# Graph network kernel: in the second network's pass the edge's part is put into the ring first, the gather adds the node's row to it, and ScalarE rectifies from the ring

## The chip, the core and the metric

The kernel runs on one core of one Trainium2 chip. The metric is the device time of one execution in microseconds (us). A core has five engines that matter here: TensorE (PE, with its weight loads as PEld), VectorE (DVE), ScalarE (ACT), GpSimd (POOL), and SyncE (SP), which here only issues DMAs. Sixteen DMA engines move the data.

## What is computed

Four graph networks run one after the other over 3125 nodes (128 features) and 50000 edges, sorted by destination. The change concerns the second one alone:

```
combined = jnp.concatenate([x[row], ef], axis=1)
msg = jax.nn.relu(combined @ Wn1 + bn1) @ Wn2 + bn2
out = jax.ops.segment_sum(msg, col, num_segments=x.shape[0])
return out + x
```

The product with `Wn1` is split in two. The node's half, `x @ Wn1[0:128] + bn1`, is a table in DRAM with a row for each node (`table`). The edge's half, `ef @ Wn1[128:]`, was computed during earlier passes and lies in DRAM by edge (`edge_part`). So each edge's message is relu(table[src] + edge_part), summed by destination; `Wn2` is applied to the sums afterwards.

## The kernel before

Edges are taken in tiles of 128, which makes 391 tiles, and four tiles make a quad (98 tile quads). A destination block is 128 nodes, and an edge tile that touches two blocks is used in two steps, so there are 416 steps in 104 step quads. All loops are unrolled, and the order is written out by hand for each engine; engines meet through semaphores (`arrived`, `mixed`, `evac`, `quad_done`, `onehot_ready`, `ring_in`, `gathered`).

The ring is a part of SBUF with 60 places, one for each tile, and every place has two halves of 128 floats. In the pass of the second network the engines do this:

- POOL (`gathers`, L479) issues one indirect DMA for each tile: it fetches 128 rows of `table`, 512 bytes each, into the first half of the tile's place. After every fourth tile it may hand over quads (`hand_over`, L470 to L475): it waits until the four gathers of a quad have landed, waits for the quad's edge load as well (`joins`, L1188), and increments `arrived`. With `rest=4` it mostly hands over the quad before the one that it has just issued; after every fourth quad, 16 tiles, it hands over the one just issued too, and stands until that has landed.
- SP (L1200) loads four tiles of `edge_part` at a time, 256 KB, into the second halves. Load k waits until quad k-8 is handed over and the place is free.
- DVE makes the one-hot matrices of a quad's destinations (L455, one instruction of 128x512) and, two quads behind that, adds the two halves of a place into `hidden` (`add`, L1209 to L1218: four instructions at L1216). Its increment of `mixed` also frees the places in the ring, for POOL (`freed`, L1185) and for SP.
- ACT rectifies a quad from `hidden` into `relu_h` in one instruction of 128x512 (L1232) and increments `evac`.
- PE adds a quad's one-hots to the degree counts (L510), one quad ahead, and multiplies relu_h with the one-hots into the block sums in PSUM (L1254).

Of the kernel before, what the change touches and what calls it, by code (L numbers as in the profile page):

```python
# [96 lines left out]
def build(nc, A, out):  # L97
    ctx = ExitStack()
    with ctx:
# [365 lines left out]

        def gathers(pool, tab, width, freed, joins=None, rest=4):

            handed = [0]

            def hand_over(k):  # L470

                pool.wait_ge(gathered[k % U].sem, gathered[k % U].at(64 * (k // U) + 16 * min(4, EDGE_TILES - 4 * k)))
                if joins is not None:
                    joins(pool, k)
                pool.sem_inc(arrived.sem, 1)  # L475
            for t in range(EDGE_TILES):
                if t % 4 == 0 and t >= RING:
                    freed(pool, (t - RING + 3 + NB - 1) // 4)
                pool.indirect_dma_start(ring[:, ds(t % RING * 2 * H, width)], None, tab,  # L479
                                        bass.IndirectOffsetOnAxis(ap=idx_s[:, t:t + 1], axis=0)).then_inc(gathered[t // 4 % U].sem, 16)  # L480
                if t % 4 == 3:
                    done = t // 4 + 1
                    for k in range(handed[0], done if done % rest == 0 else done - 1):
                        hand_over(k)
                        handed[0] = k + 1
            for k in range(handed[0], TILE_QUADS):
                hand_over(k)
# [12 lines left out]
        def step_need(eng, n):  # L500

            return eng.value_load(need_i[0:1, ds(n, 1)], min_val=1, max_val=TILE_QUADS)
# [675 lines left out]
        if STAGE >= 2:  # L1178
# [3 lines left out]
            with nc.Block() as block:  # L1182
                @block.gpsimd
                def _(pool):
                    def freed(pool, n):  # L1185
                        pool.wait_ge(mixed.sem, mixed.at(n + 1))

                    def joins(pool, k):  # L1188
                        pool.wait_ge(ring_in[k % HALF].sem, ring_in[k % HALF].at(16 * (k // HALF + 1)))
                    gathers(pool, table, H, freed, joins, rest=4)  # L1190

                @block.sync
                def _(sp):
                    pairs = ring.rearrange("p (r c) -> p r c", c=2 * H)
                    for k in range(TILE_QUADS):
                        if 4 * k >= RING:
                            sp.wait_ge(mixed.sem, mixed.at((4 * k - RING + 3 + NB - 1) // 4 + 1))
                        if k >= HALF:
                            sp.wait_ge(arrived.sem, arrived.at(k - HALF + 1))
                        sp.dma_start(pairs[:, 4 * k % RING:4 * k % RING + 4, H:2 * H],  # L1200
                                     edge_part[4 * k:4 * k + 4, :, :].rearrange("t e f -> e t f")).then_inc(ring_in[k % HALF].sem, 16)

                @block.vector
                def _(dve):
                    def join(i, q, first):
                        if not (first and q < 2):
                            add(i * QUADS + q - 2, (q - 2) % QUADS, not (first and q < 4))

                    def add(n, q, reused):  # L1209
                        r = 4 * (q % 2)  # L1210
                        slot_regs, slots, partners = step_slots(dve, n * 4, 4, behind=(0, H))
                        dve.wait_ge(arrived.sem, step_need(dve, n) + arrived.base)
                        if reused:
                            dve.wait_ge(evac.sem, evac.at(n - 1))
                        for c in range(4):
                            sum_ = dve.tensor_tensor(hidden[:, r + c, :], arena[:, ds(slots[c], H)], arena[:, ds(partners[c], H)], ALU.add)  # L1216
                        release(dve, slot_regs)
                        sum_.then_inc(mixed.sem, 1)  # L1218
                    onehots(dve, None, join, home=deep)
                    for q in range(2, QUADS):  # L1220
                        add(ALL_QUADS - QUADS + q, q, True)

                @block.scalar
                def _(act):
                    def body(i, first):
                        for q in range(QUADS):
                            n = i * QUADS + q
                            r = 4 * (q % 2)
                            act.wait_ge(mixed.sem, mixed.at(n + 1))
                            if n >= RELUS:  # L1230
                                act.wait_ge(quad_done.sem, quad_done.at(n - RELUS + 1))
                            act.activation(relu_h[:, 4 * (n % RELUS):4 * (n % RELUS) + 4, :], hidden[:, r:r + 4, :], ACT.Relu).then_inc(evac.sem, 1)  # L1232
                    trips(act, body)
                    take_totals(act)

                @block.tensor
# [23 lines left out]
                    add_totals(pe)  # L1260
            gather_pass_over()
            totals_over()
            mixed.base += ALL_QUADS
            evac.base += ALL_QUADS
            for k in range(TILE_QUADS):
                ring_in[k % HALF].base += 16
# [1128 lines left out]
```

## Time and profile before

| | us |
|---|---|
| three runs | 6473.24, 6457.61, 6471.04 (median 6471.04) |
| the profiled execution | 6410.16, its span 6408.1 |
| PE busy in the span | 3293.9 (51%) |
| POOL busy | 3221.9 (50%) |
| DVE busy | 2162.9 (34%) |
| ACT busy | 1006.4 (16%) |
| the pass of the second network, first gather to last | 2000.03 to 2566.8 of the span |

The profiled execution is one of several, and here it lies 61 us below the median of the timed ones. The shares are means over passes with different limits. An engine at half of the span can still be the one that sets the pace of a stretch, since register, semaphore and DMA-issuing instructions of the queues are not counted as busy, and the small gap between two instructions isn't either.

### The profile page before, as it was taken

To read this page: it belongs to the slowest core of one execution; us is meant where nothing else is said; L and a number is where in the kernel's file an instruction comes from. 1 tells how busy PE (TensorE), PEld (TensorE's weight loads), DVE (VectorE), ACT (ScalarE), POOL (GpSimd) and SP (SyncE) were. 2 spreads that over 40 slices of the span, in tenths; PEclk is the share of its full clock that TensorE was granted. 3 is DMA by queue.
4 is the path that set the end of the run, shared out by engine and by line. 5 is a ranking of instruction groups with operands and counts; after the bars stand their busy time and mean duration, and the time that the engine had idled before them with its cause. 6 is when DMAs were issued, how large, how long until landed. Compare 5 with 4: busy or idle time off the path is not lost. (4 is left out here: it accounts for less than half of the span.)

```text
span 6408.1 us, 51881 instructions
## 1 busy us (share of the span) xinstructions
PE 3293.9 (51%) x13857; PEld 2295.6 (36%) x13857; DVE 2162.9 (34%) x5075; ACT 1006.4 (16%) x2209; POOL 3221.9 (50%) x3406
## 2 busy tenths in 40 slices
PE   5554677767774555643463344643324356333263
PEld 3333455545552333332343232233324322333153
DVE  3222322232224222411121114533338544333485
ACT  0000322232222111200010002400004324000063
POOL 4665466546663666366646663046650320566403
PEclk7676777677776777755565556755557677555586
DMA  2111334333432332211131116976653579766453
GB/s 61 46 47 40 88 98 101 98 82 99 101 99 79 91 90 82 107 46 47 46 131 47 46 46 251 427 239 185 182 149 111 149 287 427 204 187 184 118 148 95
DMA packets 630965, 826.34 MB, mean 129 GB/s; under 512 B 93075, under 2 KB 510341, under 8 KB 618133
## 3 DMA queue, kind: packets, MB, share of 16 engines
q1 hardware_dynamic: 480117, 492.37, 22.9%
q0 software_dynamic: 120608, 276.12, 16.2%
q10 hardware_dynamic: 29952, 54.54, 2.9%
q8 instruction: 116, 1.90, 0.1%
q14 instruction: 172, 1.41, 0.1%
HBM read 470.63 MB, written 352.04 MB: 128 GB/s over the span
## 5 line engine op out<-in xcount | busy, mean ns | idle before, releaser
L479 POOL DMA_INDIRECT arena<-table,idx_s x3128 | 3001.8, 960 | 2353.5 <-issue 1095.5
L751 PE MATMUL ps<-arena,work 128*128 x4160 | 985.9, 378 | 1050.0 <-issue 934.9
L751 PEld LDWEIGHTS ps<-arena,work 128*128 128x128 f32 x4160 | 824.8, 274 | 1317.4 <-issue 1170.3
L1965 PE MATMUL ps<-arena,work 128*128 x1664 | 412.7, 426 | 693.7 <-issue 488.2
L1965 PEld LDWEIGHTS ps<-arena,work 128*128 128x128 f32 x1664 | 359.1, 317 | 748.6 <-issue 530.1
L459 DVE TENSOR_SCALAR work<-iota_row,dl_s,w_s 128x128 f32<-128x128 f32 x1248 | 350.4, 358 | 454.6 <-issue 349.4
L455 DVE TENSOR_TENSOR work<-ps,dl_s 128x512 f32<-128x512 f32 x208 | 143.8, 692 | 926.5 <-issue 617.0
L1934 DVE TENSOR_TENSOR arena<-arena,ps 128x128 f32<-128x128 f32 x832 | 182.7, 281 | 741.9 <-issue 500.0
L929 DVE SCALAR_TENSOR_TENSOR arena<-ps,vecs,arena 128x256 f32<-128x256 f32 x208 | 100.6, 484 | 893.9 <-issue 435.9
L1832 PE MATMUL ps<-arena,work 32*128 32x512 f32 x1600 | 299.1, 876 | 97.5 <-DVE work L1859 44.2
L510 PE MATMUL ps<-work,picks 128*104 128x512 f32 x416 | 313.4, 842 | 46.2 <-issue 42.8
L1863 DVE COPY arena<-ps 128x1024 f32<-128x1024 f32 x200 | 238.6, 1221 | 271.0 <-DMA table<-arena 164.8
L1254 PE MATMUL ps<-work,arena 128*128 128x128 f32 x832 | 173.5, 373 | 248.6 <-ACT arena L1232 153.7
L1654 POOL DMA_INDIRECT sorted_x<-work,pos_i x50 | 48.6, 973 | 479.8 <-DVE work L1747 465.2
L1254 PEld LDWEIGHTS ps<-work,arena 128*128 128x128 f32 x832 | 148.4, 267 | 382.4 <-ACT arena L1232 231.5
L863 PE MATMUL ps<-arena 128*128 128x128 f32 x832 | 212.3, 400 | 83.9 <-DVE arena L929 41.7
L1850 ACT ACTIVATE arena<-ps 128x1024 f32<-128x1024 f32 x200 | 198.1, 1022 | 309.7 <-DMA table<-arena 187.0
L1216 DVE TENSOR_TENSOR arena<-arena 128x128 f32 x416 | 94.7, 288 | 414.3 <-issue 245.1
L2145 PE MATMUL ps<-arena,onehot 128*128 128x128 f32 x1664 | 209.4, 280 | 21.7 <-DVE arena L2125 17.0
L863 PEld LDWEIGHTS ps<-arena 128*128 128x128 f32 x832 | 164.8, 278 | 123.0 <-DVE arena L929 64.2
L857 PE MATMUL ps<-arena 128*128 128x256 f32 x416 | 193.3, 560 | 28.9 <-ACT arena L897 25.0
L2145 PEld LDWEIGHTS ps<-arena,onehot 128*128 128x128 f32 x1664 | 194.7, 191 | 36.2 <-issue 30.7
(331 smaller groups left out, 3539.5 us busy)
## 6 DMA issues: line engine op xcount, KB each, us to landing
table<-arena SPq DMA_DIRECT2D x96, 2048.0 KB
onehot<-col_rows ACTq DMA_DIRECT2D x208, 256.0 KB
values<-arena SPq DMA_DIRECT2D x832, 64.0 KB
arena<-values SPq DMA_DIRECT2D x208, 256.0 KB
arena<-table,idx_s POOLq DMA_INDIRECT x3128
arena<-edge_times SPq DMA_DIRECT2D x208, 128.0 KB
edge_part<-arena SPq DMA_DIRECT2D x208, 128.0 KB
table<-arena SPq DMA_DIRECT2D x50, 512.0 KB
```

Source lines behind the costliest of these rows:

```text
L459: is_dst = dve.tensor_scalar(home[:, at + c, :], iota, dl_s[:, ds(j + c, 1)], weight[:, ds(j + c, 1)], ALU.is_equal, ALU.mult)
L479: pool.indirect_dma_start(ring[:, ds(t % RING * 2 * H, width)], None, tab, bass.IndirectOffsetOnAxis(ap=idx_s[:, t:t + 1], axis=0)).then_i ...
L510: mm = pe.matmul(quad_sums, picks[:, ALL_QUADS - n:2 * ALL_QUADS - n], deep[:, 4 * (n % DEEP):4 * (n % DEEP) + 4, :].rearrange("p c e -> p ...
L751: mm = pe.matmul(accf[:, ds(b, P)], o, arena[:, ds(slot, H)], start=False, stop=False, skip_group_check=True)
L857: pe.matmul(self.half_b, self.We2, self.hid[:, r, :], start=True, stop=True, skip_group_check=True).then_inc(turned.sem, 1)
L863: mm = pe.matmul(self.half_a[:, c * P:(c + 1) * P], self.ef[:, r, c * P:(c + 1) * P], self.Wn1b, start=True, stop=True, skip_group_check=True)
L1254: mm = pe.matmul(accf[:, ds(b, P)], relu_h[:, (i * U + u) % (4 * RELUS), :], o, start=False, stop=False, skip_group_check=True)
L1832: mm = pe.matmul(ps[:, 4 * kv + g, :], (value_ring if kv else key_ring)[rows, b % 2, :], (pair_v if kv else pair_k)[rows, half * 16:(half ...
L1850: act.activation(rows32[:, m % 3, :, kv * H:kv * H + 64].rearrange("p t (g c) -> p g t c", g=2), ps[:, 4 * kv:4 * kv + 2, :].rearrange("p ...
L1863: dve.tensor_copy(rows32[:, m % 3, :, kv * H + 64:(kv + 1) * H].rearrange("p t (g c) -> p g t c", g=2), ps[:, 4 * kv + 2:4 * kv + 4, :].re ...
L1965: mm = pe.matmul(ps[:, n % 8, c * P:(c + 1) * P], across_ring[:, n % DEEP, c * P:(c + 1) * P], Qn_flat[:, ds(b, P)], start=True, stop=True)
L2145: mm = pe.matmul(accf[:, ds(b, P)], o, msgs[:, 4 * q + c, :], start=False, stop=False, skip_group_check=True)
```

## The change

The halves change their order of arrival. SP now loads the edge's part into the first half of a place. POOL waits for that load before the first gather of the quad, and each gather is an indirect DMA that adds the table's row to what lies there (`compute_op: ALU.add`). Its hand-over waits for the gathers alone. DVE's adds, `hidden` and the signal `mixed` are gone from this pass; after each quad's one-hots DVE calls `release_steps`, which waits for the tile quad that a step quad needs and increments `step_ready`. ACT loads the four slot addresses of a quad into registers and rectifies straight from the ring, in four instructions of 128x128 in place of one of 128x512. `evac` now frees the places.

```diff
         def gathers(pool, tab, width, freed, joins=None, rest=4):
+            adds = {} if joins is None else {"compute_op": ALU.add}
...
                 pool.wait_ge(gathered[k % U].sem, gathered[k % U].at(64 * (k // U) + 16 * min(4, EDGE_TILES - 4 * k)))
-                if joins is not None:
-                    joins(pool, k)
                 pool.sem_inc(arrived.sem, 1)
             for t in range(EDGE_TILES):
                 if t % 4 == 0 and t >= RING:
                     freed(pool, (t - RING + 3 + NB - 1) // 4)
+                if t % 4 == 0 and joins is not None:
+                    joins(pool, t // 4)
                 pool.indirect_dma_start(ring[:, ds(t % RING * 2 * H, width)], None, tab,
-                                        bass.IndirectOffsetOnAxis(ap=idx_s[:, t:t + 1], axis=0)).then_inc(gathered[t // 4 % U].sem, 16)
+                                        bass.IndirectOffsetOnAxis(ap=idx_s[:, t:t + 1], axis=0), **adds).then_inc(gathered[t // 4 % U].sem, 16)
...
                     def freed(pool, n):
-                        pool.wait_ge(mixed.sem, mixed.at(n + 1))
+                        pool.wait_ge(evac.sem, evac.at(n + 1))
...
-                            sp.wait_ge(mixed.sem, mixed.at((4 * k - RING + 3 + NB - 1) // 4 + 1))
+                            sp.wait_ge(evac.sem, evac.at((4 * k - RING + 3 + NB - 1) // 4 + 1))
                         if k >= HALF:
                             sp.wait_ge(arrived.sem, arrived.at(k - HALF + 1))
-                        sp.dma_start(pairs[:, 4 * k % RING:4 * k % RING + 4, H:2 * H],
+                        sp.dma_start(pairs[:, 4 * k % RING:4 * k % RING + 4, 0:H],
...
-                    onehots(dve, None, join, home=deep)
-                    for q in range(2, QUADS):
-                        add(ALL_QUADS - QUADS + q, q, True)
+                    def then(i, q, first):
+                        release_steps(dve, i * QUADS + q)
+                    onehots(dve, None, then, home=deep)
...
-                            act.activation(relu_h[:, 4 * (n % RELUS):4 * (n % RELUS) + 4, :], hidden[:, r:r + 4, :], ACT.Relu).then_inc(evac.sem, 1)
+                    for n in range(ALL_QUADS):
+                        slot_regs, slots = step_slots(act, n * 4, 4)
+                        act.wait_ge(step_ready.sem, step_ready.at(n + 1))
+                        if n >= RELUS:
+                            act.wait_ge(quad_done.sem, quad_done.at(n - RELUS + 1))
+                        for c in range(4):
+                            rectified = act.activation(relu_h[:, (4 * n + c) % (4 * RELUS), :], arena[:, ds(slots[c], H)], ACT.Relu)
+                        rectified.then_inc(evac.sem, 1)
+                        release(act, slot_regs)
```

On POOL, at the start of the pass, the queue before has eight gathers without a wait, and the waits for gathers and for edge loads stand together:

```order
L479 DMA arena<-table,idx_s 128x128 x8
L479 DMA arena<-table,idx_s 128x128 [waits gathered0,ring_in0]
L479 DMA arena<-table,idx_s 128x128 x3
L479 DMA arena<-table,idx_s 128x128 [waits gathered1,ring_in1]
L479 DMA arena<-table,idx_s 128x128 x3
L479 DMA arena<-table,idx_s 128x128 [waits gathered2,ring_in2,gathered3,ring_in3]
L479 DMA arena<-table,idx_s 128x128 x7
```

The same place of the changed kernel, where L481 is the gather:

```order
L481 DMA arena<-table,idx_s 128x128 [waits ring_in0]
L481 DMA arena<-table,idx_s 128x128 x3
L481 DMA arena<-table,idx_s 128x128 [waits ring_in1]
L481 DMA arena<-table,idx_s 128x128 x3
L481 DMA arena<-table,idx_s 128x128 [waits gathered0,ring_in2]
L481 DMA arena<-table,idx_s 128x128 x3
L481 DMA arena<-table,idx_s 128x128 [waits gathered1,ring_in3]
L481 DMA arena<-table,idx_s 128x128 x3
L481 DMA arena<-table,idx_s 128x128 [waits gathered2,gathered3,ring_in4]
```

Each quad's first gather now waits for its own quad's edge load; the waits for landed gathers stand where they stood, and their number is the same.

On DVE in the middle of the pass, one turn of the loop before (L256 and L502 load the slot addresses and the need into registers):

```order
L256 TENSOR_LOAD slot_i
L502 TENSOR_LOAD need_i
L502 ISA x2
L1212 REGISTER_ALU
L1216 REGISTER_ALU [waits evac,arrived]
L1216 TENSOR_TENSOR arena<-arena 128x128
L1216 REGISTER_ALU
...
L1216 TENSOR_TENSOR arena<-arena 128x128
L455 TENSOR_TENSOR work<-iota_row,dl_s 128x512
```

and one turn in the changed kernel:

```order
L455 TENSOR_TENSOR work<-iota_row,dl_s 128x512 [waits arrived,quad_done]
L504 TENSOR_LOAD need_i
L504 ISA x2
L548 REGISTER_ALU [waits onehot_ready]
```

The one-hots (L455) now come right behind the wait for `arrived`, where the four adds stood; before, they came behind the adds.

On ACT, before and in the changed kernel, two quads:

```order
L1232 ACTIVATE arena<-arena 128x512 [waits quad_done,mixed] x94
```

```order
L256 TENSOR_LOAD slot_i
L1219 ACTIVATE arena<-arena 128x128 [waits quad_done,step_ready]
L1219 ACTIVATE arena<-arena 128x128 x3
L256 TENSOR_LOAD slot_i
L1219 ACTIVATE arena<-arena 128x128 [waits quad_done,step_ready]
```

One instruction a quad has become one load of addresses and four instructions.

## Rows read from the trace of the kernel before

**Rows 1.** The page: span, engines' busy us, DMA share by queue, all gathers.

```profile
span 6408.1 us, 51881 instructions
...
PE 3293.9 (51%) x13857; PEld 2295.6 (36%) x13857; DVE 2162.9 (34%) x5075; ACT 1006.4 (16%) x2209; POOL 3221.9 (50%) x3406
...
q0 software_dynamic: 120608, 276.12, 16.2%
...
L479 POOL DMA_INDIRECT arena<-table,idx_s x3128 | 3001.8, 960 | 2353.5 <-issue 1095.5 <-POOLq L1784 477.2 <-DMA arena<-table,idx_s 305.7
```

**Rows 2.** Stretches of this pass: busy us of each engine, PE clock, DMA share.

```profile
2050.00:2150.00 100.00, 57.68 (x182) 32.54 (x180) 27.20 (x90) 11.34 (x18) 70.42 (x70) 0.71 0.32 91
...
2250.00:2350.00 100.00, 54.96 (x180) 32.17 (x180) 28.68 (x95) 11.82 (x19) 68.42 (x68) 0.73 0.31 90
```

**Rows 3.** Groups on POOL, DVE, ACT in this pass: busy, mean ns | idle before.

```profile
L479 POOL DMA_INDIRECT arena<-table,idx_s x391 | 394.2, 1008 | 245.9 <-issue 153.7 <-POOLq L1082 73.3 <-DMA arena<-table,idx_s 18.9
...
L1216 DVE TENSOR_TENSOR arena<-arena 128x128 f32 x416 | 94.7, 288 | 414.3 <-issue 245.1 <-POOLq L475 167.5 <-ACT arena L1232 1.2
L455 DVE TENSOR_TENSOR work<-iota_row,dl_s 128x512 f32<-128x512 f32 x104 | 70.8, 683 | 2.6 <-PEq L1082 2.6
L1232 ACT ACTIVATE arena<-arena 128x512 f32<-128x512 f32 x104 | 65.5, 630 | 511.1 <-issue 335.3 <-DVE arena L1216 175.8
...
L987 ACT ACTIVATE work<-ps 128x128 f32<-128x128 f32 x1 | 0.3, 278 | 0.4 <-PE ps L965 0.4
```

**Rows 4.** Timeline of POOL: start us, us, idle before in brackets.

```profile
2251.09 0.95 POOL L479 DMA_INDIRECT arena<-table,idx_s  x1 [0.30 <-issue]
2252.35 1.31 POOL L479 DMA_INDIRECT arena<-table,idx_s  x1 [0.31 <-issue]
2256.04 1.09 POOL L479 DMA_INDIRECT arena<-table,idx_s  x1 [2.39 <-issue]
```

**Rows 5.** Timeline of POOL and DVE together, eight us further on.

```profile
2262.44 0.94 POOL L479 DMA_INDIRECT arena<-table,idx_s  x1 [0.30 <-issue]
...
2262.64 0.90 DVE L1216 TENSOR_TENSOR arena<-arena 128x128 f32 x4 [5.72 <-POOLq L475]
2263.45 0.68 DVE L455 TENSOR_TENSOR work<-iota_row,dl_s 128x512 f32<-128x512 f32 x1
...
2263.69 1.27 POOL L479 DMA_INDIRECT arena<-table,idx_s  x1 [0.30 <-issue]
```

**Rows 6.** POOL groups of two later passes: rows of 512 B, rows of 1 KB.

```profile
L479 POOL DMA_INDIRECT arena<-table,idx_s x391 | 370.5, 948 | 182.1 <-issue 143.0 <-DMA arena<-table,idx_s 23.8 <-remote 10.6
...
L479 POOL DMA_INDIRECT arena<-table,idx_s x391 | 372.9, 954 | 437.6 <-POOLq L1784 238.3 <-issue 127.6 <-DMA arena<-table,idx_s 50.4
```

**Rows 7.** One-hots (L455) of the later pass with 512 B rows.

```profile
L455 DVE TENSOR_TENSOR work<-ps,dl_s 128x512 f32<-128x512 f32 x103 | 71.2, 691 | 464.0 <-issue 322.6 <-POOLq L475 74.1 <-remote 59.2
```

**Rows 8.** Start of the pass: POOL, SP, then DMA share of two stretches.

```profile
2000.03 0.95 POOL L479 DMA_INDIRECT arena<-table,idx_s  x1 [73.29 <-POOLq L1082]
...
1999.39 12.81 SPq L1200 DMA_DIRECT2D arena<-edge_part  x10
...
1999.00:2001.00 2.00, 1.58 (x3) 0.69 (x4) 1.58 (x3) 0.00 (x0) 0.95 (x1) 0.68 0.20 49
2001.00:2003.00 2.00, 2.00 (x4) 0.96 (x3) 0.35 (x1) 0.00 (x0) 1.41 (x2) 0.50 0.96 286
```

**Rows 9.** End of the pass: POOL's last gather, then DVE, ACT and PE.

```profile
2565.84 0.95 POOL L479 DMA_INDIRECT arena<-table,idx_s  x1 [0.31 <-issue]
...
2568.72 0.90 DVE L1216 TENSOR_TENSOR arena<-arena 128x128 f32 x4 [2.90 <-POOLq L475]
2570.32 0.90 DVE L1216 TENSOR_TENSOR arena<-arena 128x128 f32 x4 [0.70 <-ACT arena L1232]
...
2571.93 1.16 PE L1254 MATMUL ps<-work,arena 128*128 128x128 f32 x8 [0.43 <-ACT arena L1232]
```

**Rows 10.** Other indirect DMAs of 128 rows: a scatter and a wider gather.

```profile
L1654 POOL DMA_INDIRECT sorted_x<-work,pos_i x50 | 48.6, 973 | 479.8 <-DVE work L1747 465.2 <-issue 14.6
L1788 POOL DMA_INDIRECT work<-sorted_kvq,pos_i x32 | 30.5, 952 | 100.6 <-POOLq L1676 91.5 <-issue 9.1
```

**Rows 11.** What SP's queue waited for in this pass: us, times, longest.

```profile
SPq L1199 <- POOLq L475: 183.9, 30, 7.7
```

More of the change, by code:

```diff
@@ L1204, in _ @@
                 def _(dve):
[L1205 to L1218, printed above, removed]
@@ L1219, in _ @@
-                    onehots(dve, None, join, home=deep)
-                    for q in range(2, QUADS):
-                        add(ALL_QUADS - QUADS + q, q, True)
+                    def then(i, q, first):
+                        release_steps(dve, i * QUADS + q)
+                    onehots(dve, None, then, home=deep)
                 @block.scalar
                 def _(act):
[L1225 to L1231, printed above, removed]
-                            act.activation(relu_h[:, 4 * (n % RELUS):4 * (n % RELUS) + 4, :], hidden[:, r:r + 4, :], ACT.Relu).then_inc(evac.sem, 1)
@@ L1233, in _ @@
-                    trips(act, body)
+                    for n in range(ALL_QUADS):
[7 more added lines that the diff above has]
+                        release(act, slot_regs)
@@ L1262, in build @@
             totals_over()
-            mixed.base += ALL_QUADS
+            step_ready.base += ALL_QUADS
             evac.base += ALL_QUADS
```

## Prediction

> **What bounds the kernel now.** I read the page first [rows 1]: no engine is busy for more than about half of the span, so the answer must come from the stretch that is changed. The pass of the second network reaches from POOL's first gather at 2000.03 us [rows 8] to its last, which starts at 2565.84 and takes 0.95 [rows 9], and that is 566.8 us. In two stretches of 100 us from its middle, PE is busy for 58 and 55 us, DVE for 27 and 29, ACT for 11 and 12, and the DMA engines have a share of 0.31 to 0.32 [rows 2]. POOL is busy for 68 to 70, and what is left of its time is explained by its own queue. The 391 gathers are busy for 394.2 us; their idle time is 245.9, of which 73.3 lie before the first [rows 3]. 394.2 + 172.6 = 566.8, so POOL's row alone fills the pass. The idle time has two parts. Between two gathers stand 0.30 to 0.31 us, and where POOL hands over the quad that it has just issued it stands for about 2.4 [rows 4]. There are 24 such places (one in 16 tiles), so the other 390 - 24 = 366 gaps hold 366 x 0.305 = 111.6 us, and the 24 long stops hold 172.6 - 111.6 = 61 us, 2.5 us each. DVE's adds wait for that hand-over (POOLq L475, 167.5 us) [rows 3], and ACT and PE wait behind DVE. They follow POOL; they do not hold it up.
>
> So an edit in this pass is worth what it does to (a) the length of a gather on POOL, (b) the 24 stops, (c) the first start and (d) the tail after the last gather.
>
> **DVE's adds go.** They are 416 x 0.288 = 94.7 us of DVE's work, plus the 0.63 us of ACT that becomes four of 0.28 us [rows 3]. DVE was waiting anyway, so in itself this is worth nothing. But it moves the one-hots, and these touch POOL. In this pass a gather takes 1008 ns in the mean, in the later pass with rows of the same size 948 [rows 3, 6]. The timeline shows which ones are longer: the adds start at 2262.64, inside the gather that started at 2262.44, and it stays at 0.94. L455 follows at 2263.45 and runs to 2264.13; the gather that starts within it, at 2263.69, takes 1.27, as if it had stood until L455 was nearly over [rows 5]. In the later pass the one-hots read their iota from PSUM (work<-ps) and the gathers are short [rows 6, 7]. After the change L455 stands where the adds stood, 0.2 us inside a gather that has already begun, and ends before the next one starts. I expect most of (1008 - 948) x 391 = 23.5 us back, and take -20; bounds -23.5 and 0.
>
> The page "SBUF — State Buffer" of the Trainium skill, section "Who interferes with whom", says that a DVE instruction with two SBUF inputs contends with a GpSimd instruction that reads SBUF. By that rule alone the adds would contend as well; the row shows them harmless at their place, so it is the start of a gather that matters, and the sum by the rule (all one-hots still have two SBUF inputs) would leave the 23.5 us where they are.
>
> **The start.** The first gather now waits for the first edge load. SP issues it at 1999.39 [rows 8]; the DMA share is 0.20 until 2001 and 0.96 in the next two us, so 256 KB are under way until about 2002. A gather's own landing takes about 2.4 us from its end [rows 4], and with as much the first gather would start at 2002.3: +2.3 us, once. Bounds +1 and +6 (all eight first loads ahead of it). Later loads are hidden: load k goes out when quad k-8 is handed over, some six quads of 5.4 us ahead of its first use, and SP's waits (184 us over the pass) [rows 11] are for exactly that hand-over. If the cover were gone, each of 98 quads would pay up to 2 us; what would be late is the first gather of a quad.
>
> **The stops.** They end when the last gather has landed. That gather now reads its destination too. The nearest row is the pass with rows of 1 KB, which moves twice the bytes in each gather: its idle time is 437.6 - 238.3 = 199.3, less 111.6 of gaps, over 24 stops 3.65 us each [rows 6], against 2.5 here. So twice the bytes cost 1.1 us a stop. I take +0.5 x 24 = +12 us; bounds 0 and +27. The DMA engines' total does not bind: the software queue holds 16.2% of them [rows 1], and twice that beside the edge loads is still under half.
>
> **The gather itself.** This decides. A gather's time on POOL is the time in which the entries for its 128 rows are written. Nothing in this trace adds in a DMA, so the cost is bounded from both sides. From below: rows of 512 B, 1 KB and 1.5 KB take 948, 954 and 952 ns, and a scatter 973 [rows 6, 10], so neither bytes nor direction count, and an adding gather could take 948 too: +0. From above: if the whole 948 ns is for entries, and all that work doubles because the destination has to be named as a source as well, +0.95 us a gather, 391 x 0.948 = +371 us. Between: entries for reading and entries for writing are two lists, an adding row needs a third entry, and if all the time is for entries it grows by half, 0.47 us, 391 x 0.47 = +184 us. Some part of 948 ns is fixed, and no row with fewer than 128 table rows tells how much. I take half of that growth, 0.24 us: +94 us. A growth of 0.05 us a gather (20 us over the pass) is enough to eat all that DVE's edit gives.
>
> Two pages of the Trainium skill speak against the change here. "Collectives: The Full Stack", section "The bandwidth ceiling: the fold count and why AG ≠ RS ≠ AR", says that the DMA's add takes two read descriptors where a copy takes one; "GPSIMD Engine Reference", section "4. When to use GPSIMD", says that of a pair of cores one writes the read descriptors and the other the write descriptors. Together they would double the longer list: the upper bound, +371 us, with nothing fixed in it. "DMA: Bandwidth & Descriptors", section "Anatomy of one DMA — SWDGE (gpsimd) path", holds that many descriptors can be written before the added cost shows: the lower bound. No run here shows either yet.
>
> **The tail.** Before, DVE starts on the last two quads at 2568.72 and 2570.32 and PE ends at 2573.1 [rows 9]. After, DVE makes one-hots (0.68) in place of adds (0.90), and ACT needs 4 x 0.28 = 1.1 us in place of 0.63: about 0, within 1 us. ACT has 5.4 us a quad, and 1.1 us plus a load of addresses fit (DVE's turn at the end, with its loads and four adds, took 1.60 [rows 9]). Where the places are freed by `evac` in place of `mixed`, it comes about 1 us later for a place that is asked for six or more quads later: nothing.
>
> **Sum.** -20 + 2 + 12 + 94 + 0 = +88 us. Against the profiled execution that is 6410 + 88 = 6498; the timed runs of the same kernel have their median 61 us above it, and the pass should shift both alike, so 6471 + 88 = 6559, say 6560. The ends of the terms give -23.5 + 1 + 0 + 0 = -22 and 0 + 6 + 27 + 371 = +404.
>
> **The rivals.**
> - *The writing of entries costs the same* (0.33 of the chance). For it: three row sizes and two directions within 3% [rows 6, 10]. Then -20 + 2 + 12 = -6 us, 6465, from -22 to +20. It ends faster by over 0.3% (19.4 us, about what a measurement of this kernel can tell from no change) only if the 60 ns come back for almost all gathers and the landings stay at 2.5 us; the stops decide at about +0.05 us each: chance 0.12 for that, 0.21 for no change.
> - *The entries cost what the upper bound says, or more* (0.12): 6471 - 20 + 2 + 27 + 371 = 6851. What speaks against it is that a scatter, whose indices are on the other list, costs only 25 ns more than a gather.
> - *The gather stays short but its landing becomes long* (0.07), because each row is read, added and written in turn: at +2 us a stop 24 x 2 = +48, 6471 - 20 + 2 + 48 = 6501. It decides from 0.8 us a stop on (19 us). The 1 KB pass shows 1.1 for double the bytes, but the edge loads compete less here.
> - *The expected moderate growth* (0.43): the sum above, from +25 to +200.
> - *The edits cancel or do nothing in the pass* (0.05), for instance because another wait of POOL fills what is saved: no change.
>
> **How the numbers follow.** Slower: 0.43 + 0.12 + 0.07 = 0.62. No change: 0.21 + 0.05 = 0.26. Faster: 0.12. The likeliest is the moderate growth, 6560, whose own range is 6496 to 6670. The range for 8 in 10 leaves out half of the upper rival and the fast end of the first: 6452 to 6760.
>
> **What would show each step.** POOL's group of gathers in this pass: mean 948 ns if entries cost nothing, 1.19 us as I take it, 1.9 at the bound; if it is over 1.25 us the pass is over 600 us long. The stops: 2.5 us against 3.0. The first gather should start 2 to 3 us after the first edge load is issued. L455 should no longer sit across a gather's start; if gathers that start inside it stay long, the first term is wrong. If a quad's first gather waits for `ring_in` in the middle of the pass, the loads are not hidden and I have missed a term. PE, ACT and DVE should all still wait for POOL; if ACT is the one waited for, its loads of addresses cost more than I think.

## The result, and the profile after

The changed kernel takes 6698.41 us in the median of 4 runs (6690.45 to 6706.79), the kernel before 6464.32 in 4 runs on the same chip (6445.94 to 6473.24). The ratio is 1.0366, interval 1.0338 to 1.0394: slower by 234 us. I had forecast 6560 (+88), range 6452 to 6760.

The page of the changed kernel, to be laid beside [rows 1]:

```profile
span 6696.6 us, 51446 instructions
...
PE 3332.4 (50%) x13857; PEld 2341.3 (35%) x13857; DVE 2077.6 (31%) x4659; ACT 1035.6 (15%) x2521; POOL 3446.9 (51%) x3406
...
q0 software_dynamic: 164400, 276.12, 17.3%
...
L481 POOL DMA_INDIRECT arena<-table,idx_s x3128 | 3227.9, 1032 | 2376.6 <-issue 1064.8
```

POOL's gathers are busy for 226 us more, with as many instructions as before. DVE has 416 adds less. The software queue moves the same 276.12 MB in 43792 more packets, which is 112 for each of the 391 gathers of this pass.

The pass itself, by groups with shapes kept apart (busy, mean ns | idle before), and two stretches of 100 us from its middle, as in [rows 3] and [rows 2]:

```profile
L481 POOL DMA_INDIRECT arena<-table,idx_s x391 | 627.7, 1605 | 249.0 <-issue 106.0 <-DMA arena<-edge_part 74.0 <-DMA arena<-table,idx_s 69.0
```

```profile
L1219 ACT ACTIVATE arena<-arena 128x128 f32 x416 | 94.4, 297 | 719.3 <-DVEq L549 719.2
L455 DVE TENSOR_TENSOR work<-iota_row,dl_s 128x512 f32<-128x512 f32 x104 | 72.0, 692 | 739.1 <-POOLq L475 735.3 <-PEq L1084 2.6 <-DVE work L455 1.2
```

```profile
2100.00:2200.00 100.00, 48.02 (x137) 30.84 (x136) 9.00 (x13) 11.79 (x52) 78.08 (x50) 0.62 0.38 64
2300.00:2400.00 100.00, 47.16 (x130) 30.01 (x130) 8.99 (x13) 11.80 (x52) 77.31 (x48) 0.62 0.38 64
```

The gathers' busy time went from 394.2 us [rows 3] to 627.7. The idle time inside the pass was 172.6 and is 249.0 - 74.0 = 175.0. Together 802.7 us in place of 566.8, and these 235.9 us are as much as the medians differ by (234). The two profiled executions differ by 288 us; the other 52 lie outside this pass, 43 of them behind the seventh of the eight gather passes (from its last gather to the next pass 712.8 us in place of 687.5, and from the very last gather to the end 387.6 in place of 370.3), where the change touches nothing. The likely reason is that the profile before was taken on another chip than the timed runs: its 6410 us lies 36 us under the fastest of the four and inside the 6403 to 6439 that the same kernel took on a second chip. The pass can be compared all the same: on two chips (those of the experiments below) passes of adding gathers took 783.4 and 784.0 us, and copying gathers of 128 rows have medians of 944 to 955 ns in every trace. In 100 us POOL issues 48 to 50 gathers, where it had issued 68 to 70. DVE waits for POOL's hand-over for 735 of the pass's 803 us, and ACT and PE wait behind DVE. So POOL's row alone still fills the pass.

All gathers of this pass by their line: shortest, median and longest, then what their engine waited for. The same view of the kernel before follows.

```profile
L481 POOL DMA_INDIRECT arena<-table,idx_s x391: 1531/1540/2028, 2006.8 to 2808.0; - x196
its engine sat idle before it (us, times) until:
  issue: 106.0, 348
  DMA arena<-edge_part: 74.0, 1
  DMA arena<-table,idx_s: 69.0, 42
```

```profile
L479 POOL DMA_INDIRECT arena<-table,idx_s x391: 941/947/1447, 2000.0 to 2565.8; - x196
```

The shortest rose by 590 ns and the median by 593: so this is no wait that some of them meet; each one is longer by the same amount. 391 x 0.593 = 232 us. Some are longer still: 76 of the 391 start while L455 runs and take 334 ns more than the median on average, 25 us together. The other 315 stay at the median. (In the kernel before, 72 started while L455 ran, for 23 us.) The edge loads are waited for once, ahead of the first gather.

A quad in the timeline, on ACT, DVE and POOL, and the start of the pass, as in [rows 5] and [rows 8]:

```profile
2309.63 1.54 POOL L481 DMA_INDIRECT arena<-table,idx_s  x1 [0.30 <-issue]
2311.21 0.91 ACT L1219 ACTIVATE arena<-arena 128x128 f32 x4 [7.94 <-DVEq L549]
2311.27 0.69 DVE L455 TENSOR_TENSOR work<-iota_row,dl_s 128x512 f32<-128x512 f32 x1 [8.15 <-POOLq L475]
2311.48 1.89 POOL L481 DMA_INDIRECT arena<-table,idx_s  x1 [0.30 <-issue]
```

```profile
2003.70 5.37 SPq L1202 DMA_DIRECT2D arena<-edge_part  x8
2006.82 1.59 POOL L481 DMA_INDIRECT arena<-table,idx_s  x1 [74.02 <-DMA arena<-edge_part]
```

L455 starts 0.10 us after the end of the first gather shown (2311.17), where DVE's adds had started 0.50 after it (2262.64 against 2262.14 [rows 5]). The next gather begins at 2311.48, 0.2 us *inside* the one-hots, and takes 1.89 in place of 1.54.

### The profile page after: what moved, and what is told of

The parts are those of the page before. It is cut to its first block and busy times, and to the rows that moved or that the text cites. A ratio compares the mean times of both kernels' runs of the same rounds, so it can differ in the third digit from the quotient of the medians.

```text
span 6696.6 us, 51446 instructions
## 1 busy us (share of the span) xinstructions
PE 3332.4 (50%) x13857; PEld 2341.3 (35%) x13857; DVE 2077.6 (31%) x4659; ACT 1035.6 (15%) x2521; POOL 3446.9 (51%) x3406
## 3 DMA queue, kind: packets, MB, share of 16 engines
q0 software_dynamic: 164400, 276.12, 17.3%
## 5 line engine op out<-in xcount | busy, mean ns | idle before, releaser
L481 POOL DMA_INDIRECT arena<-table,idx_s x3128 | 3227.9, 1032 | 2376.6 <-issue 1064.8
L753 PE MATMUL ps<-arena,work 128*128 x4160 | 971.3, 374 | 1008.8 <-issue 919.7
L753 PEld LDWEIGHTS ps<-arena,work 128*128 128x128 f32 x4160 | 820.8, 272 | 1259.3 <-issue 1146.7
L1953 PE MATMUL ps<-arena,work 128*128 x1664 | 405.7, 403 | 700.2 <-issue 591.1
L1953 PEld LDWEIGHTS ps<-arena,work 128*128 128x128 f32 x1664 | 346.5, 297 | 760.4 <-issue 640.5
L512 PE MATMUL ps<-work,picks 128*104 128x512 f32 x416 | 353.5, 939 | 477.9 <-DVE work L455 430.4
L455 DVE TENSOR_TENSOR work<-ps,dl_s 128x512 f32<-128x512 f32 x208 | 143.9, 692 | 930.3 <-issue 674.0
L455 DVE TENSOR_TENSOR work<-iota_row,dl_s 128x512 f32<-128x512 f32 x104 | 72.0, 692 | 739.1 <-POOLq L475 735.3
L512 PEld LDWEIGHTS ps<-work,picks 128*104 128x104 f32 x416 | 81.8, 240 | 521.7 <-DVE work L455 457.4
L1242 PEld LDWEIGHTS ps<-work,arena 128*128 128x128 f32 x832 | 197.2, 325 | 108.6 <-issue 108.6
```

The lines of the kernel that those rows point to most:

```text
L455: is_dst = dve.tensor_tensor(home[:, at:at + 4, :], iota.unsqueeze(1).to_broadcast([P, 4, P]), dl_s[:, ds(j, 4)].unsqueeze(2).to_broadcast ...
L512: mm = pe.matmul(quad_sums, picks[:, ALL_QUADS - n:2 * ALL_QUADS - n], deep[:, 4 * (n % DEEP):4 * (n % DEEP) + 4, :].rearrange("p c e -> p ...
L753: mm = pe.matmul(accf[:, ds(b, P)], o, arena[:, ds(slot, H)], start=False, stop=False, skip_group_check=True)
L1242: mm = pe.matmul(accf[:, ds(b, P)], relu_h[:, (i * U + u) % (4 * RELUS), :], o, start=False, stop=False, skip_group_check=True)
L1953: mm = pe.matmul(ps[:, n % 8, c * P:(c + 1) * P], across_ring[:, n % DEEP, c * P:(c + 1) * P], Qn_flat[:, ds(b, P)], start=True, stop=True)
```

## The experiments

Two things had to be told apart: what the add costs each gather, and what the one-hots' place does. Theory A: a gather that adds takes about 0.59 us more on POOL whatever stands around it, and DVE delays a gather only where an instruction with two inputs in SBUF lies across its start. The rivals put the loss on the other parts of the change (the order of the loads, DVE's and ACT's new work), on contention over the whole length of the gather, or on the bytes that are now read twice. Each kernel was timed beside the kernel before on the same chip. That kernel takes 6412, 6459 and 6348 us on the three chips of these experiments (the last in one run), so total times are only compared on one chip; the lengths of gathers and of the pass are compared across chips.

**The change without the add.** In the changed kernel:

```diff
-            adds = {} if joins is None else {"compute_op": ALU.add}
+            adds = {}
```

> The changed kernel with its gathers in this pass copying instead of adding, so the edge's part is overwritten and missing from the result; everything else of the change stays. Theory A (the add makes each gather's time on POOL longer, 948 to 1540 ns at least): gathers return to a mean of 950 to 1010 ns, the pass to 566 to 572 us, the kernel to 0 to 6 us above the kernel before, about 6468. Rival B (the wait for the edge load ahead of each quad, or ACT's four instructions and address loads, hold the ring): the pass stays above 650 us and the gaps between gathers grow.

Measured: 6431.76 us (10 runs) against 6412.32, ratio 1.0032, 1.0010 to 1.0053. Its gathers in the pass:

```profile
L481 POOL DMA_INDIRECT arena<-table,idx_s x391 | 375.0, 959 | 256.5 <-issue 160.3 <-DMA arena<-edge_part 75.0 <-DMA arena<-table,idx_s 12.8
```

Everything else of the change is in it, and the pass takes 556.6 us, 246 less than with the add. The whole kernel is still not faster than before. The pass is 10 us shorter than the one of before, but PE is late at its end: from the last gather to the first of the next pass 99.8 us go by, against 85.5. (PE is the subject of the last section.) That makes 4 us more; the rest of the 19 between the medians isn't located, and the profiled execution (6414.75) is the fastest of the ten.

**The add without the rest.** In the kernel before, only the gathers of this pass add (to what lies in the ring, so the sums are other ones, with the same work), and DVE's adds stay:

```diff
+            adds = {} if joins is None else {"compute_op": ALU.add}
...
-                                        bass.IndirectOffsetOnAxis(ap=idx_s[:, t:t + 1], axis=0)).then_inc(gathered[t // 4 % U].sem, 16)
+                                        bass.IndirectOffsetOnAxis(ap=idx_s[:, t:t + 1], axis=0), **adds).then_inc(gathered[t // 4 % U].sem, 16)
```

> The kernel before with nothing changed but that the gathers of this pass add to what lies in the ring (rows of an older tile, so the messages hold those as well). Theory A (the add is the whole loss; the order of loads, ACT's part and DVE's release cost nothing beside gathers this slow): mean of the gathers 1600 ns with the adds of DVE in their old place or 1545 to 1560 where the one-hots then miss a gather's start; the pass 780 to 800 us, the kernel 215 to 235 us over the kernel before. Rival B (a good part of the loss is in the rest of the change): the kernel less than 190 us over the kernel before.

Measured: 6666.06 us (4 runs) against 6458.56, ratio 1.0331, 1.0311 to 1.0352.

```profile
L480 POOL DMA_INDIRECT arena<-table,idx_s x391 | 608.8, 1557 | 246.3 <-issue 106.6 <-POOLq L1083 71.7 <-DMA arena<-table,idx_s 68.0
```

This one argument is worth 207 of the 234 us. The pass is 783.4 us long, 19 less than in the changed kernel, and all of the difference is in the gathers (608.8 against 627.7). Their median is the same, 1541 ns against 1540; only fewer are delayed, although DVE does more: five start inside L455 and not 76.

**One-hots from one SBUF tensor.** In the changed kernel, four instructions of 128x128 take the place of one of 128x512, with the destination number as a scalar:

```diff
+                    if weight is None and single:
+                        for c in range(4):
+                            is_dst = dve.tensor_scalar(home[:, at + c, :], iota, dl_s[:, ds(j + c, 1)], None, ALU.is_equal)
...
-                    onehots(dve, None, then, home=deep)
+                    onehots(dve, None, then, home=deep, single=True)
```

> The changed kernel with the one-hots of a quad made by four TENSOR_SCALAR instructions of 128x128 (one SBUF tensor and a column as scalar) in place of one TENSOR_TENSOR with two SBUF inputs. Theory A (a gather that starts while a DVE instruction reads two SBUF inputs stands until that is nearly over; one in four does, 0.35 us each): the mean of the gathers falls from 1605 to 1540 to 1550 ns, the pass by 22 to 26 us, the kernel to about 6675. Rival B (the long gathers come with the hand-over itself, whatever DVE does): the mean stays at 1600, the time at 6698. Rival C (TENSOR_SCALAR blocks POOL's writes too): the mean rises above 1605.

Measured: 6619.56 us (4 runs) against 6412.32, ratio 1.0319, 1.0298 to 1.0339.

```profile
L484 POOL DMA_INDIRECT arena<-table,idx_s x391 | 603.0, 1542 | 250.1 <-issue 106.0 <-DMA arena<-edge_part 74.8 <-DMA arena<-table,idx_s 69.2
```

The mean falls on the median, and the pass is 24.4 us shorter, at the same idle time. That is the delay by the one-hots, seen alone: 96 gathers still start while DVE makes one-hots, and they lie 6 ns over the median on average.

**DVE's adds back in their place.** Four adds ahead of the next one-hots, whose result nobody reads:

```diff
                         release_steps(dve, i * QUADS + q)
+                        for c in range(4):
+                            dve.tensor_tensor(hidden[:, c, :], iota_row[:, :], iota_row[:, :], ALU.add)
```

> The changed kernel with four additions of 128x128 by DVE ahead of each quad's one-hots, where they stood before; they add the iota row to itself and nothing uses the result. Theory A (only what lies across a gather's start counts): the one-hots move 0.8 us back, from 0.2 us ahead of a gather's start to the middle of a gather of 1540 ns; the additions now lie across the start and cost up to 0.2 us each time, so the mean falls from 1605 to 1545 to 1590 ns. Rival B (each DVE instruction with two SBUF inputs costs POOL its own time): 94 us more of them, and the mean rises towards 1700 ns or more.

Measured in one run: 6642.96 us, the pass 784.0. Its gathers as a group, and a quad of its timeline:

```profile
L481 POOL DMA_INDIRECT arena<-table,idx_s x391 | 608.7, 1557 | 250.9 <-issue 108.5 <-DMA arena<-edge_part 75.6 <-DMA arena<-table,idx_s 66.9
```

```profile
2312.79 0.91 DVE L1210 TENSOR_TENSOR arena<-iota_row 128x128 f32<-128x128 f32 x4 [6.07 <-POOLq L475]
2312.97 1.54 POOL L481 DMA_INDIRECT arena<-table,idx_s  x1 [0.30 <-issue]
2313.62 0.68 DVE L455 TENSOR_TENSOR work<-iota_row,dl_s 128x512 f32<-128x512 f32 x1
```

More work on DVE made the pass 19 us shorter. The adds too lie across the gather's start here, but each is short (0.9 us for four), and this gather is not held (1.54). Others are, by little: 97 start inside an add alone and lie 39 ns over the median on average, 4 us in all; only four still start inside the one-hots and are held for 0.5 us. The one-hots now fall inside the gather and do no harm, with the same two SBUF inputs as before, and they are not longer themselves (0.68). Contention over the gather's whole length is ruled out. The last experiment below agrees: in it L455 begins inside 68 gathers that had started before it, and these are at the median.

**The scalar one-hots in the kernel before.** The same edit there:

> The kernel before with the one-hots of this pass made by four TENSOR_SCALAR instructions of 128x128 in place of one TENSOR_TENSOR. Theory A (a gather that starts inside a DVE instruction with two SBUF inputs stands until that is nearly over, and TENSOR_SCALAR with one does not hold it): the gathers' mean falls from 1008 to 948 to 955 ns, the pass from 566.8 to 543 to 548 us, the kernel by 18 to 24 us. Rival B (the longer DVE work, 4 x 0.36 us in place of 0.68, delays DVE's adds, which were on the heels of POOL): the pass gains less than 8 us.

Measured: 6484.83 us (8 runs) against 6458.56, ratio 1.0035, 1.0012 to 1.0058.

```profile
L482 POOL DMA_INDIRECT arena<-table,idx_s x411 | 392.1, 954 | 277.7 <-issue 150.2 <-POOLq L1085 69.5 <-DVE arena L1219 30.9
```

(The group holds 20 gathers of the pass ahead.) The gathers became short, 954 ns in place of 1008, but the pass did not: 571.0 us in place of 566.8. The 21 us that came off the gathers went into waits for free places (DVE's adds, L1219, 30.9 us). The mechanism holds, the gain that I expected doesn't. Whether DVE's longer one-hots or PE (last section) made the places late, this run doesn't separate.

**No stops.** In the kernel before, the argument that makes POOL rest every fourth quad:

```diff
-                    gathers(pool, table, H, freed, joins, rest=4)
+                    gathers(pool, table, H, freed, joins, rest=1000)
```

> The kernel before with rest=1000 in this pass: POOL never hands over the quad that it has just issued, so the 24 stops for a landing go, and every fourth quad is handed over four gathers later. Theory A (the stops are plain loss to the engine that sets the pace): 24 x 2.1 = 50 us less in the pass, the kernel about 50 us faster. Rival B (POOL needs the stops for something else, such as room for its descriptors, and the time comes back in longer gathers or gaps): less than 20 us gained, and the mean or the gaps between gathers grow.

Measured: 6474.14 us (12 runs) against 6458.56, ratio 1.0030, 1.0014 to 1.0045, the pass 569.0.

```profile
L479 POOL DMA_INDIRECT arena<-table,idx_s x391 | 389.2, 996 | 251.8 <-issue 109.8 <-POOLq L1082 72.0 <-DVE arena L1216 64.5
```

A miss. The stops' 61 us did not come back: POOL now waits 64.5 us for the same ring places that DVE frees. So "POOL's row alone fills the pass" was true of the kernel before, but with little to spare: a quicker POOL meets the next limit at once.

**Fewer rows.** Each gather takes fewer indices, so that part of the rows is missing: 64 rows in the first pass and 32 in the next two, copying, and 64 in this one, adding. The ring is set to zero once, at the start.

```diff
-                pool.indirect_dma_start(ring[:, ds(t % RING * 2 * H, width)], None, tab,
-                                        bass.IndirectOffsetOnAxis(ap=idx_s[:, t:t + 1], axis=0), **adds).then_inc(gathered[t // 4 % U].sem, 16)
+                pool.indirect_dma_start(ring[0:rows, ds(t % RING * 2 * H, width)], None, tab,
+                                        bass.IndirectOffsetOnAxis(ap=idx_s[0:rows, t:t + 1], axis=0), **adds).then_inc(gathered[t // 4 % U].sem, 16)
```

> The changed kernel with gathers of fewer rows, so that parts of the messages are missing: 64 of 128 rows in the first pass (copying), 32 in the next two passes (copying), 64 in the second network's pass (adding). Theory A (a fixed part, and a part for each entry; the add needs a second read entry for each row): with 128 rows 947 copying and 1540 adding; 64 rows copying 600 to 800, adding 0.30 us more than that, so 900 to 1100; 32 rows lie on the line through the copying ones. Rival B (the add has a fixed surcharge, such as another code path): adding with 64 rows stays 0.55 to 0.6 us above copying with 64. Rival C (all of the time is for rows, nothing fixed): 474 and 237 ns copying, 770 adding.

The second kernel of this kind takes 8, 16, and 16 rows:

> The changed kernel with still fewer rows a gather, so that most of the messages is missing: 8 rows in the first pass (copying), 16 in the next two (copying), 16 in the second network's pass (adding). So far: 944, 907 and 870 ns for 128, 64 and 32 rows copying, 1540 and 1422 for 128 and 64 adding. Theory A (a straight line for each: about 0.6 ns a row over 850 to 870 copying, 1.85 ns a row over 1300 adding, so the add is mostly a surcharge that the number of rows does not change): 16 rows copying 855 to 865, 8 rows the same within 20 ns, 16 rows adding 1310 to 1345. Rival B (the surcharge is for each DMA engine that takes part and shrinks with them, or the curve bends): 16 rows adding under 1200.

Measured in one run each: 6677.63 and 6667.12 us. The totals say little, since in both the pass starts 67 and 80 us later than in the changed kernel. The gathers' lengths are what counts (shortest, median, longest). The adding pass and passes 0, then 1 and 2 of the first kernel:

```profile
L481 POOL DMA_INDIRECT arena<-table,idx_s x391: 1412/1422/1856, 2073.9 to 2817.9; - x196
...
L481 POOL DMA_INDIRECT arena<-table,idx_s x343: 901/907/1061, 75.2 to 559.1; - x172
...
L481 POOL DMA_INDIRECT arena<-table,idx_s x826: 864/870/1003, 559.1 to 1949.3; - x166
```

The same of the second kernel:

```profile
L481 POOL DMA_INDIRECT arena<-table,idx_s x391: 1304/1309/1800, 2087.3 to 2778.6; - x196
...
L481 POOL DMA_INDIRECT arena<-table,idx_s x344: 856/860/1046, 74.6 to 559.8; - x172
...
L481 POOL DMA_INDIRECT arena<-table,idx_s x816: 841/847/962, 559.8 to 1949.4; - x164
```

| rows of a gather | copying, ns | adding, ns | more by |
|---|---|---|---|
| 8 | 860 | | |
| 16 | 847 | 1309 | 462 |
| 32 | 870 | | |
| 64 | 907 | 1422 | 515 |
| 128 | 947 | 1540 | 593 |

Of a copying gather's 947 ns some 0.84 us are there with hardly any rows. The add's surcharge goes from 462 to 593 ns over 112 rows, so 1.2 ns for each row, and by the straight line a fixed 462 - 16 x 1.2 = 443 ns, 0.44 us. Three quarters of the loss don't grow with the rows. This was not the make-up that theory A had: 64 rows copying were to take 600 to 800 ns, and adding 0.30 us more. Rival B, a fixed surcharge of 0.55 to 0.6, is nearer. The second kernel came out within 8 ns of what the first had led me to expect.

**Half of the bytes.** The gathers of this pass add 64 numbers a row and not 128; half of each sum is missing.

```diff
-                    gathers(pool, table, H, freed, joins, rest=4)
+                    gathers(pool, table.rearrange("n (a f) -> (n a) f", a=2), H // 2, freed, joins, rest=4)
```

> The changed kernel with gathers of this pass that add 64 floats (256 bytes) a row in place of 128, from a table read as twice as many half rows; half of each message has the edge's part alone and the other half a wrong node's. Theory A (what the add costs on POOL is a surcharge for the instruction and a little for each row, and bytes don't count): a gather takes 1530 to 1550 ns as with 512 bytes, the pass stays at 795 to 805 us; the 24 stops may shrink by 0.1 to 0.3 us each. Rival B (POOL's time holds part of the data's movement, since an adding row is a packet of its own): the mean falls by over 0.1 us, below 1500 ns.

Measured in one run: 6581.80 us, beside 6347.78 for one of the kernel before, the pass 789.2.

```profile
L481 POOL DMA_INDIRECT arena<-table,idx_s x391: 1532/1541/1845, 1983.5 to 2771.2; - x196
```

1541 ns against 1540: the bytes don't count. The pass is 14 us shorter than in the changed kernel, which I had not expected (795 to 805): fewer gathers start inside L455 with a long delay (15 us in all in place of 25), and the waits for landings are 60.4 us in place of 69.0.

## Why the prediction was wrong in size

**What bounds the pass** was right: POOL's own queue, before and after. The sign was right too; I had given it 0.62.

**The gather itself.** This is the step that failed, as a term that was mis-sized. The prediction put it as "Some part of 948 ns is fixed, and no row with fewer than 128 table rows tells how much. I take half of that growth, 0.24 us: +94 us." It measured 0.593 us and 232 us. I had thought of the surcharge as a third list of entries, in proportion to the rows, and shrank it for the fixed part. The runs show the opposite make-up: the fixed part of a copy is nearly all of it (0.84 of 0.947), its rows are almost free, and the add brings a fixed part of its own, 0.44 us, beside 1.2 ns a row. What the fixed 0.44 us is made of, the runs don't tell. The bounds, 0 and 0.95, held it. So the result fell between two rivals: over the moderate growth, whose range ended at 6670, and under the upper bound's 6851. The mark that the prediction had set, over 1.25 us a gather and over 600 us for the pass, was passed by both.

The Trainium skill's rule of two read descriptors for an add ("Collectives: The Full Stack", "The bandwidth ceiling: the fold count and why AG ≠ RS ≠ AR") had given +371 us. The runs show 0.63 of that, and since three quarters of it don't grow with rows, a longer list can be behind the last quarter at most. The other page ("DMA: Bandwidth & Descriptors", "Anatomy of one DMA — SWDGE (gpsimd) path"), by which descriptors are cheap to write, agrees for a copy (100 ns from 16 to 128 rows) and would have put the add at nothing, which is wrong.

What the DMA side does is seen in the packets of the software queue (packets, MB, share of 16 engines) of this pass, the kernel before and then the changed one:

```profile
q0 software_dynamic: 12480, 25.58, 16.2%
```

```profile
q0 software_dynamic: 56160, 25.58, 26.4%
```

For 390 gathers that is 32 packets each before and 144 after. A copy had its 128 rows in packets of several rows, 16 beside 16 small ones, and the add has one packet for each row. The engines' share stays at a quarter, and POOL's waits for landings grew by 2.4 us over the pass (the stops, below). The fixed part is not a matter of packets: an adding gather of 16 rows has 32 of them (12480 for 390), as many as a copy of 128 rows, and takes 1309 ns against 947. With 64 rows it has 80 (31200 for 390), with 128 it has 144, so the part that grows goes with rows and packets alike; whether it is the price of writing these is only argued.

**DVE's adds go** (-20) failed. The prediction put it as "After the change L455 stands where the adds stood, 0.2 us inside a gather that has already begun". It stands 0.2 us ahead of one, since DVE answers POOL's hand-over 0.4 us sooner with the one-hots than it had with the adds. The gathers' mean lies 1605 - 1540 = 65 ns above their median, as it lay 1008 - 947 = 61 above it before: +2 us in place of -20. That a delay arises only at a gather's start was right, and three experiments show it: 24.4 us go when the one-hots read one SBUF tensor, 19 when the adds push them past the start, 19 when the kernel before adds in its gathers. The size of the delay fits too. Here the one-hots end at 2311.96, 0.48 us after the gather's start, and it is 0.35 us too long; in [rows 5] they end at 2264.13, 0.44 after the start, and it is 1.27 - 0.95 = 0.32 too long. The rule of "SBUF — State Buffer", section "Who interferes with whom", in the Trainium skill names the right pair of instructions and gave this term's true result (0). Taken as a rule for any overlap it would be too wide: the same pair, with the gather 0.65 us under way, costs neither of them anything (1.54 and 0.68 us).

**The stops** (+12): 175.0 - 111.6 = 63.4 us against 61.0, +2.4, 0.1 us a stop. The row that I had scaled from, of gathers with 1 KB rows, was the wrong neighbour; why its stops are longer was not looked into. The rival of long landings fell with it.

**The start** (+2): the first gather starts 3.1 us after the first edge load is issued, and not 0.64: +2.5. Later loads are hidden, as forecast.

**The tail** (0): from the last gather's end to the end of PE's L1242 it took 2573.09 - 2566.79 = 6.3 us; after, 7.3. Right to within its 1 us.

With the measured terms: 232 + 2 + 2.4 + 2.5 + 1 = 240, and the medians give 234.

**The hidden rival.** The case that nothing is added to the gather was to give 6465, a gain of 6 us, and the first experiment is that case: it came out 19 us slower than before (ratio 1.0010 to 1.0053). So on that chip even a free add would have brought nothing. Its profile shows PE falling behind, but no run has this kernel without that, and on a chip where PE doesn't (last section) it was not tried.

## What to carry to other kernels

An indirect DMA of 128 rows costs POOL hardly more than one of 16 (947 ns against 847), so price an edit to it by measuring one with few rows and one with many; a term that is fixed does not shrink because there is little to move. Moving arithmetic from an engine that waits into the queue that everybody waits for costs its whole price, here 0.59 us each time, and can gain no more than the waiting engine's work had cost the queue, here at most 24 us. And where a short conflict depends on which instruction starts first, 0.4 us of reaction decide it: what a moved instruction will stand beside has to be worked out from the hand-over to its start, not from the place of the instruction that it replaces.

## What the runs showed of the hardware that was not expected

That an adding gather costs 0.44 us more with almost no rows, 1.2 ns more for each row and nothing for bytes, is told above. The other thing is PE's. In the kernel with quicker gathers (the change without the add), PE does this for long stretches:

```profile
2149.95 0.29 PEld L1242 LDWEIGHTS ps<-work,arena 128*128 128x128 f32 x1 [2.50 <-issue]
2150.65 0.37 PE L1242 MATMUL ps<-work,arena 128*128 128x128 f32 x1 [1.72 <-issue]
2151.35 0.29 PEld L1242 LDWEIGHTS ps<-work,arena 128*128 128x128 f32 x1 [1.12 <-issue]
2153.45 0.37 PE L1242 MATMUL ps<-work,arena 128*128 128x128 f32 x1 [2.43 <-issue]
```

One instruction starts every 0.70 us or a multiple of it, though each takes 0.3 to 0.4, and the engine waits for nothing that the profile shows. No records are missing: all 832 matmuls of L1242 are there, and in between PE catches up (221 matmuls from 2160 to 2210 us). The windows of this kernel and then of the kernel before, over the same 50 us:

```profile
2060.00:2110.00 50.00, 10.14 (x20) 5.58 (x20) 6.23 (x9) 7.26 (x32) 34.72 (x37) 0.50 0.33 95
```

```profile
2060.00:2110.00 50.00, 30.60 (x100) 16.96 (x100) 13.68 (x46) 5.67 (x9) 35.20 (x36) 0.68 0.31 91
```

The granted clock is 0.50 there, the lower of the two levels, and PE is busy for a third as long. POOL issues as many gathers, and ahead of it the ring fills, until DVE and ACT wait for PE. Two waits of the whole pass in the change without the add (us, times, longest):

```profile
DVE work L455 <- PE ps L1242: 136.0, 26, 20.3
ACT arena L1219 <- PE ps L1242: 136.0, 24, 20.1
```

In this pass such stretches come in the three kernels whose gathers are quicker or don't rest (this one, the scalar one-hots in the kernel before, no stops), and in none that adds, nor in the kernel before. In other passes ten of the eleven traces have them. The eleventh is the half-width kernel, profiled on the chip where the kernel before takes 6348 us: starts of PE that lie 1.39 to 1.42 us behind the one before come 304 to 572 times in the ten, and once in it. Below are fifty us of the first pass, whose work is the same in both, for the kernel before and then for the half-width kernel:

```profile
275.00:325.00 50.00, 15.69 (x36) 9.28 (x37) 9.04 (x32) 0.00 (x0) 32.88 (x35) 0.50 0.17 46
```

```profile
275.00:325.00 50.00, 30.59 (x94) 16.55 (x94) 10.74 (x39) 0.00 (x0) 34.54 (x37) 0.67 0.18 48
```

The lower clock alone doesn't make such a stretch: in a later pass the half-width kernel has it as well, and PE does 105 matmuls in 50 us.

```profile
3050.00:3100.00 50.00, 25.49 (x105) 22.83 (x105) 6.92 (x10) 0.00 (x0) 34.80 (x37) 0.50 0.19 49
```

So the chip seems to matter, as far as one run can tell; what starts the stretches is open. They are the likely reason why none of the three kernels beat the kernel before, read from the waits above and not from a run without them. No version that was faster was found on the chips where they come; on the other one none was tried.
